# Running the last layers of three narrow batch tiles once, on 512 columns

## The reference

```python
e = stack([tbl_f[ids[:, f]] for f in range(32)], axis=1)          # 2048 x 32 x 64
z = sum(e, axis=-1)                                               # 2048 x 32
outer = einsum('bpd,pde,bpe->bp', e[:, II, :], kernels, e[:, JJ, :])   # 2048 x 496
h = concatenate([z, outer, dense_ctx], axis=1)                    # 2048 x 544
h = maximum(h @ W_top1 + b_top1, 0)                               # 512 wide
h = maximum(h @ W_top2 + b_top2, 0)                               # 256 wide
y = h @ W_top3                                                    # 2048 x 1
```

## Time and profile before

| | |
|---|---|
| executions | 868.46, 868.84, 869.98 us, median 868.84 |
| profiled execution | time 869.06 us, span 867.2 us |
| PE, VectorE, POOL, ACT busy | 842.1, 622.6, 483.9, 151.9 us |
| steps (L610) on PE | 476.7 us in 2976 matmuls |
| sums (L627) on PE | 239.4 us in 2976 matmuls |
| gathers (L365) on POOL | 512, mean 944 ns each |
| tile 3 begins on PE | at 240.3 us |

### The profile page before, as it was taken

How to read it: one execution, slowest core, us unless ns; L and a number is a source line. 1 busy time by engine, 2 the same in 40 slices (tenths; PEclk the granted TensorE clock), 3 DMA queues, 4 the chain that set the end, 5 groups by cost and what they waited for, 6 DMA issues and landing times.

```text
span 867.2 us, 15755 instructions
## 1 busy us (share of the span) xinstructions
PE 842.1 (97%) x6584; PEld 403.7 (47%) x6584; DVE 622.6 (72%) x706; ACT 151.9 (18%) x273; POOL 483.9 (56%) x518
## 2 busy tenths in 40 slices
PE   2999999999999999999999999999999999999998
PEld 1888888776645333333333333333333333333333
DVE  1776677688865888888855488888855678888850
ACT  1222312212311220120210320020111212011002
POOL 6765777777777777777776477667733430000000
PEclk9999999999999999999999999999999999999999
DMA  9511111111111111111111011111100000000000
GB/s 327 195 25 25 27 32 28 27 29 30 27 28 26 28 28 26 31 27 26 28 26 25 16 24 26 25 25 26 26 13 13 14 16 1 1 1 1 1 1 1
DMA packets 24353, 28.32 MB, mean 33 GB/s; under 512 B 13398, under 2 KB 13657, under 8 KB 24156
## 3 DMA queue, kind: packets, MB, share of 16 engines
q0 software_dynamic: 16384, 16.81, 9.8%
q1 hardware_dynamic: 7888, 10.49, 3.6%
q10 hardware_dynamic: 12, 0.01, 0.0%
HBM read 27.27 MB, written 0.01 MB: 31 GB/s over the span
## 4 chain that ended last, share of the span: by engine, by line
PE 95%; DVE 2%; DMA 1%; issue 1%; POOL 1%; ACT 0%; DVEq 0%; ACTq 0%
PE y L610 52%; PE acc L627 26%; PE y L657 5%; PE y L593 4%; PE y L685 3%; DVE prod L558 2%; PE y L668 2%; PE y L662 1%; PE y L698 1%; POOL rows L365 1%; DMA rows<-tbl,ids_sb 1%; PE y L639 0%; DMA ids_sb<-ids 0%; DVEq L259 0%; ACT h L478 0%
## 5 line engine op out<-in xcount | busy, mean ns | idle before, releaser
L558 DVE TENSOR_TENSOR prod<-y,xt 128x1024 f32<-128x1024 f32 (+2 forms) x600 | 581.8, 1031 | 198.3 <-PE y L610 197.3
L365 POOL DMA_INDIRECT rows<-tbl,ids_sb x512 | 483.2, 944 | 222.8 <-issue 112.1
L610 PE MATMUL y<-xt,kw 64*128 64x512 f32 (+2 forms) x2976 | 476.7, 462 | 4.7 <-DVE prod L558 3.5
L610 PEld LDWEIGHTS y<-xt,kw 64*128 64x128 f32 x2976 | 242.7, 189 | 219.3 <-issue 201.9
L627 PE MATMUL acc<-prod,ones_strip 128*32 128x512 f32 (+2 forms) x2976 | 239.4, 454 | 0.3 <-DVE prod L558 0.3
L627 PEld LDWEIGHTS acc<-prod,ones_strip 128*32 128x32 f32 x2976 | 79.4, 109 | 142.4 <-issue 68.1
L411 ACT COPY xt<-y 128x1024 f32<-128x1024 f32 (+3 forms) x56 | 36.2, 646 | 297.0 <-PE y L593 296.9
L593 PE MATMUL y<-ident,rows 128*128 128x128 f32 x256 | 41.2, 288 | 16.2 <-DMA rows<-tbl,ids_sb 16.1
L530 DVE TENSOR_REDUCE z_rows<-rows 128x8 f32<-128x512 f32 (+2 forms) x96 | 44.5, 497 | 15.0 <-DMA rows<-tbl,ids_sb 15.0
L442 ACT COPY h_in<-acc 128x512 f32<-128x512 f32 (+2 forms) x24 | 10.6, 443 | 240.4 <-PE acc L627 240.4
L593 PEld LDWEIGHTS y<-ident,rows 128*128 128x128 f32 x256 | 28.0, 142 | 40.8 <-issue 32.6
(11 more groups left out here) (23 smaller groups left out, 66.7 us busy)
## 6 DMA issues: line engine op xcount, KB each, us to landing
rows<-tbl,ids_sb POOLq DMA_INDIRECT x512, 2.4
kw<-pair_k SPq DMA_DIRECT2D x14, 512.0 KB, 11.4
w_sb<-w SPq DMA_DIRECT2D x1, 1024.0 KB
w_sb<-w SPq DMA_DIRECT2D x1, 512.0 KB
kw<-pair_k SPq DMA_DIRECT2D x1, 384.0 KB
kw<-pair_k SPq DMA_DIRECT2D x1, 256.0 KB, 3.9
w1z_sb<-w1z SPq DMA_DIRECT2D x1, 256.0 KB
ids_sb<-ids SPq DMA_DIRECT2D x1, 240.0 KB, 2.7
```

The lines of the kernel that those rows point to most:

```text
L365: pool.indirect_dma_start(out=rows[:, s, c, h, :], out_offset=None, in_=tables[f], in_offset=bass.IndirectOffsetOnAxis(ap=ids_sb[:, b, f:f ...
L558: nc.vector.tensor_tensor(prod_part(t, d, n), y_part(t, d, n), x, ALU.mult).then_inc(y_read, n)
L610: last = nc.tensor.matmul(y[:, h, :], kw[part, d, :], xt[part, slot_of(t, units[h][0] // 2), 0:w], start=True, stop=True)
```

## The change

The layers of tiles 0, 1 and 2 no longer run each in the tile behind. Their inputs `h_in` and `z_in` are collected side by side in 512 columns, and the layers run once for the three, in tile 3. `MLP_TILES` lists which tiles share a run, `mlp_of` gives the run of a tile and its columns. The wide tiles keep their own runs, and all four runs are 512 columns wide; the output is stored four times and not six.

The couples of tile 3 are transposed at other steps than before: couples 0 and 2 at steps 92 and 108 of tile 2 (before: 84 and 100), couple 4 at step 2 of tile 3 (before: step 116 of tile 2), couple 6 at step 12 (before: 8). Each number stands for a pair of couples. All other transposes and the transposes of the field sums (`fields`, step 76, in tile 0 step 108) stay where they were, and so do the steps of the layers in tiles 3 to 5.

```diff
+MLP_TILES = [[0, 1, 2], [3], [4], [5]]
+assert all(sum(WIDTHS[t] for t in tiles) == TILE for tiles in MLP_TILES)
+
+def mlp_of(t):
+    m = next(m for m, tiles in enumerate(MLP_TILES) if t in tiles)
+    first = sum(WIDTHS[b] for b in MLP_TILES[m] if b < t)
+    return m, slice(first, first + WIDTHS[t])
+
+FIRST_WIDE = WIDTHS.index(TILE)
+
+def visits_ahead(t):
+    if t == 1:
+        return [(0, 112), (2, 116), (4, 120)]
+    return [(0, 92), (2, 108)] if t == FIRST_WIDE else [(0, 84), (2, 100), (4, 116)]
+
+def visits(t):
+    return ([(4, 2), (6, 12)] if t == FIRST_WIDE else [(6, 8)]) + [(8, 20), (10, 36), (12, 56), (14, 72)]
...
@@ later_tile_work(t)
-    for j, d in enumerate(PAIR_STEPS):
-        n = COUPLES * t + AHEAD + 2 * j
-        if n < COUPLES * TILES:
-            work[d // p * p].append(("couples", *divmod(n, COUPLES)))
-        if AHEAD + 2 * j == COUPLES - 2:
-            work[d // p * p + 4].append(("fields", t, 0))
-    for d, what in zip(MLP_STEPS, (("mlp1", t - 1, 0), ("mlp1", t - 1, 1), ("mlp2", t - 1, 0), ("mlp3", t - 1, 0))):
-        work[groups(t)[1] + d].append(what)
+    for k, d in visits(t):
+        work[d // p * p].append(("couples", t, k))
+    work[76].append(("fields", t, 0))
+    if t + 1 < TILES:
+        for k, d in visits_ahead(t + 1):
+            work[d // p * p].append(("couples", t + 1, k))
+    m, _ = mlp_of(t - 1)
+    if t - 1 == MLP_TILES[m][-1]:
+        for d, what in zip(MLP_STEPS, (("mlp1", m, 0), ("mlp1", m, 1), ("mlp2", m, 0), ("mlp3", m, 0))):
+            work[groups(t)[1] + d].append(what)
...
@@ read_acc(t, c), read_fields(t)
-                if t > 0:
-                    act.wait_ge(y_full, y_use("mlp1", t - 1, 1) + 1)
+                m, cols = mlp_of(t)
+                if m > 0:
+                    act.wait_ge(y_full, y_use("mlp1", m - 1, 1) + 1)
-                nc.scalar.copy(h_in[:, c, 0:w], accs[(CHUNKS * t + c) % 2][:, 0:w]).then_inc(acc_read, 1)
+                nc.scalar.copy(h_in[:, c, cols], accs[(CHUNKS * t + c) % 2][:, 0:w]).then_inc(acc_read, 1)
...
-                nc.scalar.copy(z_in[:, 0:w], y_banks[u % Y_SLOTS][:, 0, 0:w]).then_inc(act_read, 1)
+                nc.scalar.copy(z_in[:, cols], y_banks[u % Y_SLOTS][:, 0, 0:w]).then_inc(act_read, 1)
...
@@ mlp1, on PE (mlp2, mlp3 and the reads on ScalarE change in the same way: m for t, all 512 columns for 0:w)
-                    pe.wait_ge(act_read, act_uses_through(y_use("fields", t, 0)))
-                    pe.wait_ge(acc_read, CHUNKS * (t + 1) - 1)
+                    pe.wait_ge(act_read, act_uses_through(y_use("fields", MLP_TILES[m][-1], 0)))
+                    pe.wait_ge(acc_read, CHUNKS * (MLP_TILES[m][-1] + 1) - 1)
...
-                        nc.tensor.matmul(y[:, h, 0:w], w1_sb[:, c, j * P:(j + 1) * P], h_in[:, c, 0:w],
+                        nc.tensor.matmul(y[:, h, :], w1_sb[:, c, j * P:(j + 1) * P], h_in[:, c, :],
```

More of the change, by code:

```diff
@@ L142, in first_tile_work @@
         work[d // p * p].append(("extra", 0, s))
-    for j in range(0, AHEAD, 2):
-        work[N_STEPS - 2 * (AHEAD - j)].append(("couples", 1, j))
-    work[N_STEPS - 2 * AHEAD - 4].append(("fields", 0, 0))
+    for k, d in visits_ahead(1):
+        work[d].append(("couples", 1, k))
+    work[108].append(("fields", 0, 0))
     return work
@@ L181, in plan @@
         order.append(("sum", t, len(groups(t)) - 2))
-        order += [("mlp1", t, 0), ("mlp1", t, 1), ("mlp2", t, 0), ("mlp3", t, 0)]
+        m, _ = mlp_of(t)
+        order += [("mlp1", m, 0), ("mlp1", m, 1), ("mlp2", m, 0), ("mlp3", m, 0)]
     return order
@@ L446, in read_fields, with read_mlp1 @@
                 w = WIDTHS[t]
+                _, cols = mlp_of(t)
                 act.wait_ge(y_full, u + 1)
-                nc.scalar.copy(z_in[:, 0:w], y_banks[u % Y_SLOTS][:, 0, 0:w]).then_inc(act_read, 1)
[L451 to L454, removed]
+                nc.scalar.copy(z_in[:, cols], y_banks[u % Y_SLOTS][:, 0, 0:w]).then_inc(act_read, 1)
+            def read_mlp1(m, pair):
+                u = y_use("mlp1", m, pair)
+                if m == 0 and pair == 0:
                     act.wait_ge(small_loaded, 48)
                 elif pair == 0:
-                    act.wait_ge(y_full, y_use("mlp2", t - 1, 0) + 1)
-                    act.wait_ge(out_stored, 16 * t)
+                    act.wait_ge(y_full, y_use("mlp2", m - 1, 0) + 1)
+                    act.wait_ge(out_stored, 16 * m)
                 act.wait_ge(y_full, u + 1)
@@ L465, in read_mlp1, with read_mlp2, read_mlp3 @@
                     j = 2 * pair + h
-                    nc.scalar.activation(h1[:, j, 0:w], y_banks[u % Y_SLOTS][:, h, 0:w], ACT.Relu,
+                    nc.scalar.activation(h1[:, j, :], y_banks[u % Y_SLOTS][:, h, :], ACT.Relu,
                                          bias=b1_sb[:, j:j + 1]).then_inc(done, 1)
[L469 to L474, removed]
+            def read_mlp2(m):
+                u = y_use("mlp2", m, 0)
+                if m > 0:
+                    act.wait_ge(y_full, y_use("mlp3", m - 1, 0) + 1)
                 act.wait_ge(y_full, u + 1)
                 for j, done in enumerate((half_read, act_read)):
-                    nc.scalar.activation(h2[:, j, 0:w], y_banks[u % Y_SLOTS][:, j, 0:w], ACT.Relu,
+                    nc.scalar.activation(h2[:, j, :], y_banks[u % Y_SLOTS][:, j, :], ACT.Relu,
                                          bias=b2_sb[:, j:j + 1]).then_inc(done, 1)
-            def read_mlp3(t):
-                u = y_use("mlp3", t, 0)
-                w = WIDTHS[t]
+            def read_mlp3(m):
+                u = y_use("mlp3", m, 0)
                 act.wait_ge(y_full, u + 1)
-                nc.scalar.copy(h1[0:1, 0, 0:w], y_banks[u % Y_SLOTS][0:1, 0, 0:w]).then_inc(act_read, 1)
+                nc.scalar.copy(h1[0:1, 0, :], y_banks[u % Y_SLOTS][0:1, 0, :]).then_inc(act_read, 1)
                 act.wait_ge(act_read, act_uses_through(u))
-                act.dma_start(out[0:1, P * first_block(t):P * first_block(t) + w], h1[0:1, 0, 0:w]
+                act.dma_start(out[0:1, TILE * m:TILE * m + TILE], h1[0:1, 0, :]
                               ).then_inc(out_stored, 16)
@@ L508, in _ @@
                     read_mlp3(t)
-            act.wait_ge(out_stored, 16 * TILES)
+            act.wait_ge(out_stored, 16 * len(MLP_TILES))
         @block.vector
@@ L641, in transpose_fields, with mlp1 @@
                 last.then_inc(y_full, 1)
-            def mlp1(t, pair):
+            def mlp1(m, pair):
                 if pair == 0:
-                    if t == 0:
+                    if m == 0:
                         pe.wait_ge(weights_loaded, 48)
-                    pe.wait_ge(act_read, act_uses_through(y_use("fields", t, 0)))
-                    pe.wait_ge(acc_read, CHUNKS * (t + 1) - 1)
-                w = WIDTHS[t]
-                y = take_y(y_use("mlp1", t, pair))
+                    pe.wait_ge(act_read, act_uses_through(y_use("fields", MLP_TILES[m][-1], 0)))
+                    pe.wait_ge(acc_read, CHUNKS * (MLP_TILES[m][-1] + 1) - 1)
+                y = take_y(y_use("mlp1", m, pair))
                 for h in range(2):
@@ L661, in mlp1, with mlp2 @@
                     j = 2 * pair + h
-                    nc.tensor.matmul(y[:, h, 0:w], w1z_sb[part, j * P:(j + 1) * P], z_in[part, 0:w],
+                    nc.tensor.matmul(y[:, h, :], w1z_sb[part, j * P:(j + 1) * P], z_in[part, :],
                                      start=False, stop=False)
-                pe.wait_ge(acc_read, CHUNKS * (t + 1))
+                pe.wait_ge(acc_read, CHUNKS * (MLP_TILES[m][-1] + 1))
                 for h in range(2):
                     j = 2 * pair + h
-                    last = nc.tensor.matmul(y[:, h, 0:w], w1_sb[:, CHUNKS - 1, j * P:(j + 1) * P],
-                                            h_in[:, CHUNKS - 1, 0:w], start=False, stop=True)
+                    last = nc.tensor.matmul(y[:, h, :], w1_sb[:, CHUNKS - 1, j * P:(j + 1) * P],
+                                            h_in[:, CHUNKS - 1, :], start=False, stop=True)
                 last.then_inc(y_full, 1)
-            def mlp2(t):
-                u = y_use("mlp2", t, 0)
-                w = WIDTHS[t]
+            def mlp2(m):
+                u = y_use("mlp2", m, 0)
                 for c in range(J1):
                     if c % 2 == 0:
-                        pe.wait_ge(half_read, 3 * t + c // 2 + 1)
+                        pe.wait_ge(half_read, 3 * m + c // 2 + 1)
                     else:
-                        pe.wait_ge(act_read, act_uses_through(y_use("mlp1", t, c // 2)))
+                        pe.wait_ge(act_read, act_uses_through(y_use("mlp1", m, c // 2)))
                     if c == 0:
@@ L684, in mlp2, with mlp3 @@
                     for j in range(J2):
-                        last = nc.tensor.matmul(y[:, j, 0:w], w2_sb[:, c, j * P:(j + 1) * P], h1[:, c, 0:w],
+                        last = nc.tensor.matmul(y[:, j, :], w2_sb[:, c, j * P:(j + 1) * P], h1[:, c, :],
```

(7 more changed lines are left out.)

2 lines of the change are left out of this document (removed).

## The result

The changed kernel takes 872.76 us (median of 6 runs, 870.45 to 873.77), the kernel before 868.92 us (6 runs, 868.39 to 869.98). The ratio is 1.0041, 95% interval 1.0027 to 1.0054: slower by 3.8 us. The profiled execution took 873.77 us with a span of 872.0, against 869.06 and 867.2; it is the slowest of the six.

A forecast was written before the change was run, and what follows sets the result against it. TensorE, 97% busy, bounds the kernel, with saturated GpSimd gathers as second clock. Of 15.6 us gained, two waits take 5.8, leaving 9.9; 11.9 more layer work makes +2.0: 871.0 us, own range 870.0 to 871.8, wide 869.4 to 874.8.

The forecast's parts named there:

- The waits: TensorE waits for gathers: 1.8 us at step 108 of tile 2, 4.0 us at step 2 of tile 3.
- The work: Layers of tiles 0 to 2 merged in tile 3: 3.7 us less TensorE work, but 11.9 us more in tile 3.
- the third rival: VectorE becomes the bound in the narrow tiles 1 and 2; with 8 us lost, 873.2 us; chance 0.05.
- the second: Rival: gathers are no limit at tile 3's couples, so the gain of fewer instructions remains: 866.1 us, faster; chance 0.10.
- The sum: At tile 3: step 2 starts 9.9 us earlier, then 11.9 us more layer work, so 2.0 us later after layer 3.
- the wide one: Range for the whole kernel's time, 869.4 to 874.8 us, leaving out gathers no limit and the clock case's far end.
- the first rival: TensorE's clock drops to half in the 4.0 us wait in tile 3, costing 3 us: 874.0 us; chance 0.17.
- The sign that the prediction names: Clock drop shows if the 16 step instructions behind tile 3's wait for gathers take over 3.7 us.

## Why the prediction was right, and where it fell short

**The waits.** Right in place and size: 1.80 us from 209.75 on and 3.69 from 227.83 on, where the prediction has 1.8 from 210.0 and 4.0 from 227.8. PE came to step 108 at 209.09 (209.5 said) and to step 2 at 227.18 (227.3), and the last transposes began at 231.52 (231.8), which is POOL's earlier start.

**The work.** Right: the layers on 512 columns took 8.33, 8.12, 6.87 and 1.70 us, 11.8 us more than those of tile 2, where 11.9 was said. PE's waits for products are 0.8 us in three places as before, where I took 1 us more, so the third rival is out, and the second fell with the two waits.

**The sum.** I forecast +2.0 us and the likeliest time of 871.0. The median of 872.76 lies above the forecast's own range (870.0 to 871.8) and inside the wide one only because that one made room for the clock. The profiled execution is 4.7 us above that of before. Of these 2.9 are the clock: 0.45 in the transposes, 1.9 in steps 2 and 3, 0.6 in the sum. The other 1.8 are the forecast's own. For the median of the six runs, 3.8 us, that leaves 2.0 for the clock. The runs spread over 3.3 us, those of the kernel before over 1.6; the granted clocks of 0.996 and 0.998 explain up to 1.7 us of that (half of the difference between 7.0 and 3.5 us), and the rest is not traced.

**The step that was undersized** is the clock behind the wait. The prediction had it as a rival at 0.17 and 3 us, not as a term of the sum, because the trace of before had no idle stretch of that length between dense matmuls. So both mechanisms were at work together, the forecast's and the first rival's. The price was near (2.9 us in the profiled execution, 2.0 in the median), the chance was far too low: the clock fell in all six executions, and in 12 of 12 built-in bare waits of 4.6 us and more. The sign that the prediction names, over 3.7 us for 16 step instructions, was misjudged: only eight stand between the wait and the sum, and these alone took 3.79 us.

**What the runs don't show.** That 12 slots free the gain of the merged layers, and that filling the real wait brings the changed kernel to 871, were expected and are untested where the two waits exist. So the part of the two waits in the lost gain rests on the trace of one execution and on its balance, not on a run without them. That couples 2 to 5 had to move as late as they did is also untested there: with the old places the prediction's method gives waits of 7.6 and 7.9 us.

## What to carry to other kernels

Where one engine is busy for 97% and another runs at its own full rate beside it, work removed from the first counts only until it meets the second: take the next transfers' landing times from the trace and look for the smallest margin (here 0.5 us) before adding up the work. Work moved from ahead of such a meeting point to behind it is not saved, it is added. And a wait of some 4 us between matmuls should be priced with 2 us on top of its length (1.4 to 2.9 in these traces).

## What was unexpected of the hardware

- After an idle stretch of 4.6 to 6.9 us the granted clock was half in all 12 cases, for the next 3 to 6 us of matmuls. For shorter stretches length alone did not decide: 2.04 us once with a fall (granted clock 0.50 from 903 to 905 us), 3.48 us once without (1.00 from 970 to 980 us), 3.69 us (the changed kernel) with, 1.8 and 1.2 without. The Trainium skill, "TensorE: Matmul & The Clock Gate", section "HAM oscillation", says of waits for transfers that the array falls back to the half clock in them, and these traces agree. Its part on PE-mode transpose says that transposes do not count as activity in the same way; of that 2.1 us per wait among steps and 2.2 among transposes show nothing.
- The kernel before took 869 us on some chips and 1147 to 1160 on others. In the changed kernel's trace on such a chip PE waits 100 us for nothing that the profile shows, nearly all of it in the tiles of 128 and 256 columns, and the granted clock averages 0.75 from 100 to 450 us, where on the first chip the kernel before has 1.00.
